# A two-layer cross-attention kernel: the second attention's row maxima two steps earlier, and its tokens turned inside the first MLP

## The reference, cut to what matters

```
x = layer0(x, ctx)                 # 512 queries, 64 keys, 16 heads of 32; then LN, MLP 512->2048->512
# layer 1: queries are the 512 tokens of x ("latents"); keys and values are ctx (64 rows) and x (512 rows)
h = concatenate([ctx, x])
q = latents @ q_w + q_b ; k, v = h @ kv_w + kv_b
p = softmax(where(mask, q k^T / 32, -inf))          # 16 heads, 512 x 576 scores each
y = (p v) @ out_w + out_b + latents
out = gelu(rmsnorm(y) @ mlp_w1 + mlp_b1) @ mlp_w2 + mlp_b2 + latents
```

## Time and profile before

| | us |
|---|---|
| median of 3 runs | 1754.24 (1750.44 to 1754.75) |
| profiled execution, its own time | 1764.97 |
| its span, first to last instruction | 1763.2 |
| attention1 in it | 699 to 1382 |
| mean granted TensorE clock | 0.951 |

### The profile page before, as it was taken

The page is one execution under the profiler, slowest core; times in us unless marked ns, Lnnn a source line. Parts: engine busy times, 40 slices in busy tenths (PEclk is TensorE's granted clock), DMA queues, the critical chain, the costliest instruction groups (busy, mean ns, idle before and its releaser), DMA issues.

```text
span 1763.2 us, 23342 instructions
## 1 busy us (share of the span) xinstructions
PE 1611.1 (91%) x7033; PEld 1212.9 (69%) x7033; DVE 972.0 (55%) x1657; ACT 689.6 (39%) x1243; POOL 556.5 (32%) x543
## 2 busy tenths in 40 slices
PE   5778787989999999899999999999988899999998
PEld 4667675667787777666666666666643677887886
DVE  4665656564333333377757675776787574333333
ACT  3443333342111111178647755883766342111110
POOL 3231236501213140444514433451466401313000
PEclk9788988999999999899999899999986999999999
DMA  5001104500001032723322323322221510001011
GB/s 186 1 30 43 59 24 143 209 13 22 27 18 30 18 115 81 212 66 109 104 76 77 117 64 105 97 86 91 86 74 54 198 36 21 27 16 32 0 48 48
DMA packets 60410, 126.18 MB, mean 72 GB/s; under 512 B 9989, under 2 KB 10378, under 8 KB 60322
## 3 DMA queue, kind: packets, MB, share of 16 engines
q1 hardware_dynamic: 53282, 102.13, 17.5%
q0 software_dynamic: 7040, 23.07, 4.2%
HBM read 90.25 MB, written 34.60 MB: 71 GB/s over the span
## 4 chain that ended last, share of the span: by engine, by line
PE 74%; DVE 12%; issue 6%; ACT 5%; DMA 2%; POOL 0%; SPq 0%; DVEq 0%; ACTq 0%; POOLq 0%
PE bank L2221 19%; PE bank L2233 19%; PE bank L2068 6%; PE bank L2104 4%; DVE RA L1365 4%; PE bank L2119 3%; PE bank L2120 3%; PE bank L2081 3%; PE bank L2128 3%; PE bank L2064 2%; PE bank L1866 2%; PE bank L1890 2%; PE bank L1941 1%; PE bank L1930 1%; DMA RA<-rows_ 1%
## 5 line engine op out<-in xcount | busy, mean ns | idle before, releaser
L2233 PE MATMUL bank<-W,RA 128*128 128x512 f32 x1536 | 379.7, 399 | 5.9 <-DVE RA L1365 5.6
L2221 PE MATMUL bank<-RA,W 128*128 (+1 forms) x1536 | 374.8, 396 | 2.9 <-issue 2.3
L2233 PEld LDWEIGHTS bank<-W,RA 128*128 128x128 f32 x1536 | 287.3, 189 | 78.2 <-DVE RA L1365 10.5
L928 POOL TENSOR_TENSOR RA<-FA,RA 128x512 fp32r<-128x512 f32 (+1 forms) x160 | 233.7, 1463 | 339.7 <-ACT FA L1191 338.7
L2221 PEld LDWEIGHTS bank<-RA,W 128*128 128x128 f32 x1536 | 286.9, 188 | 75.1 <-issue 6.1
L1257 ACT ACTIVATE FA<-bank,cols 128x512 f32<-128x512 f32 x128 | 88.2, 689 | 542.0 <-PE bank L2221 541.9
L1768 DVE CAST RA<-FA 128x512 fp32r<-128x512 f32 x128 | 63.6, 497 | 354.7 <-ACT FA L1257 354.7
L1190 ACT ACTIVATE RA<-bank 128x512 fp32r<-128x512 f32 (+1 forms) x320 | 192.7, 602 | 148.7 <-PE bank L2104 136.3
L1604 DVE TENSOR_REDUCE FA<-bank 128x1 f32<-128x512 f32 x256 | 174.0, 685 | 102.6 <-PE bank L2081 97.1
L1365 DVE TENSOR_TENSOR RA<-FA,RA 128x512 fp32r<-128x512 f32 (+1 forms) x292 | 223.0, 764 | 9.0 <-ACT FA L1191 2.4
L1191 ACT ACTIVATE FA<-bank 128x512 f32<-128x512 f32 (+1 forms) x320 | 191.5, 599 | 0.0
(11 more groups left out here) (154 smaller groups left out, 1829.7 us busy)
## 6 DMA issues: line engine op xcount, KB each, us to landing
RA<-k_parts SPq DMA_DIRECT2D x96, 144.0 KB
FA<-after_layer SPq DMA_DIRECT2D x12, 1024.0 KB, 6.0
RA<-q_parts SPq DMA_DIRECT2D x96, 128.0 KB
k_parts<-FA SPq DMA_DIRECT2D x16, 576.0 KB, 2.8
after_att<-FA SPq DMA_DIRECT2D x32, 256.0 KB, 2.1
q_parts<-FA SPq DMA_DIRECT2D x16, 512.0 KB, 2.6
raw<-in_L_xattn_mlp_w_dram POOLq DMA_DIRECT2D x32, 256.0 KB, 3.4
RA<-after_att SPq DMA_DIRECT2D x10, 512.0 KB, 7.0
```

Of the source, the lines that this page charges most:

```text
L928: pool.tensor_tensor(pl[0:m, r, :], pf[0:m, r, :], ph[0:m, r, :].bitcast(F32), ALU.subtract).then_inc(p_lo_pool, 1)
L2221: op = pe.matmul(bank[FC1_BANK[i]][:, :], W[:, slot, a, k, i * P:(i + 1) * P], yT_[:, ds(b * (2 * KT * S) + (d * KT + k) * S, S)], start=( ...
L2233: op = pe.matmul(bank[4 + t][:, :], gs[:, a, i, t * P:(t + 1) * P], W[:, slot + 1, d, i, :], start=(i == 0 and a == 0 and d == 0), stop=(i ...
```

## The change

Four things are done at once.

1. `SHIFT`, `TURN` = 5, 15 in place of 7, 17: every `max_step` stands two steps earlier, and both rows of maxima are turned two steps earlier. The fillers are laid anew: Q in steps 0 to 3, K in 6 to 11, KC in 12 and 13; in group c = 1 Q in 0 to 3, K in 6 to 8, KC in 9, nC in 17. The opening has 15 max_steps in place of 13.
2. The copy of the turned maxima (`max_turned`) goes from VectorE to ScalarE, ahead of the exponentials of the step after the turn. It waits also for the bank use before it to be freed.
3. TensorE's turning of the tokens leaves attention1. Group 3 of the first MLP is written out in place of a loop, and while batch b (1 to 3) is at work in it, TensorE turns batch b-1 out of `acc_` (`x_turn`, four transposes after each of fc1(1), fc2(0), fc1(2), fc2(1); bank 3), ScalarE moves it out (`x_out`), and SP stores it to the new DRAM tensor `x_turned` (`x_store`); batch 0 goes straight into `xT`, with VectorE writing its lo part (`x_lo`). Batch 3 is turned in the opening, in front of nKC0 and nK1 (banks 2 and 3), stored from there.
4. In group c = 1 the turned tokens of the next batch are loaded into `tokT`; ScalarE writes the hi part (steps 11, 13, 15, 17) and GpSimd the lo part (`x_split`, in its order behind steps 12, 14, 16 and 18) from SBUF. No PSUM bank is used. TensorE waits for the four of them before nQ0, the filler of step 0 of group c = 2.

```diff
-TURN = 17
-SHIFT = 7
+TURN = 15
+SHIFT = 5
...
-    spans = ((0, 3), (3, 3), (8, 1)) if turns else ((0, 6), (8, 6), (14, 2))
+    spans = ((0, 4), (6, 3), (9, 1)) if turns else ((0, 4), (6, 6), (12, 2))
...
-        plan += [(s0, 1, f"nT{k}") for k, s0 in enumerate((9, 11, 13, 15))] + [(18, 1, "nC")]
+        plan += [(s0, 1, f"nT{k}") for k, s0 in enumerate((10, 12, 14, 16))] + [(17, 1, "nC")]
...
-FIRST = ([f"nT{k}" for k in range(KT)] + ["nC", "nQ0", "nK0", "nKC0", "nQ1", "nK1", "nKC1"]
+FIRST = (["nC", "nQ0", "nK0", "nKC0", "nQ1", "nK1", "nKC1"]
...
+FIRST_X = {"nKC0": (0, 1), "nK1": (2, 3)}
...
+            def x_store(nb, k):
+                sp.wait_ge(x_moved, KT * nb + k + 1 + ONE)
+                sp.dma_start(x_turned[nb, :, k, :], x_stage[nb][k]).then_inc(x_stored[k % 2], 16)
...
+                        if not last and n // NSTEP == 1:
+                            for s0, _, u in fillers(1, last):
+                                if u[:2] == "nT" and n % NSTEP == s0 + 2:
+
+                                    k = int(u[2:])
+                                    wait_apart(pool, (act_out, at(0, b, SPLITS, split1(u, last) + 1)))
+                                    pool.tensor_tensor(xT[:, 1, k, :], tokT[:, k, :], xT[:, 0, k, :].bitcast(F32),
+                                                       ALU.subtract).then_inc(x_split, 1)
...
+                def max_turned(b, u, nb, c, pair, last=False, first=False):
+                    n = use1(u, last, first)
+                    wait_apart(act, (pb_full, at(0, b, USES, n + 1)), (pb_free, at(0, b, USES, n)),
+                               (maxed[c % 2][pair], at(0, nb, 32, 16 * (c // 2))))
+                    act.activation(nT[:, c % 2, pair, :], bank[n % 2][0:H // 2, 0:P], ACT.Copy).then_inc(pb_free, 1)
...
+            def x_turn(nb, k):
+
+                if k == 0:
+                    pe.wait_ge(acc_added, (NGRP - 1) * B * TT + (nb + 1) * TT + ONE)
+                pe.wait_ge(x_moved, KT * nb + k - (nb == B - 1 and k > 0) + ONE)
+                for t in range(TT):
+                    at_t = nb * TT * D + t * D + k * P
+                    op = pe.transpose(bank[3 if nb < B - 1 else 2 + k % 2][:, t * P:(t + 1) * P],
+                                      acc_[:, at_t:at_t + P], ident[:, :])
+                op.then_inc(x_full, 1)
...
-                            wait_apart(pe, (pb_free, at(0, b, USES, use1("nC", last) + 1)))
+                            wait_apart(pe, (pb_free, at(0, b, USES, use1("nC", last) + 1)), (x_split, at(0, b, KT, KT)))
```

More of the change, by code:

```diff
@@ L1242, in attention1 @@
                 act.activation(cols[:, NPAR + 3:NPAR + 4], cols[:, NPAR:NPAR + 1], ACT.Exp)
-                for u in split_by_act(FIRST):
-                    hi(0, u, first=True)
+                for u in FIRST:
+                    for k in FIRST_X.get(u, ()):
+                        x_out(B - 1, k)
+                    if u == "nR00":
+                        max_turned(0, u, 0, 0, 0, first=True)
+                    else:
+                        hi(0, u, first=True)
+                for i in range(2):
+                    act.wait_ge(x_stored[i], 16 * (B - 1) * KT // 2 + ONE)
                 with act.Fori(0, B - 1) as b:
@@ L1274, in mlp @@
                 for g in range(1, NGRP):
-                    with act.Fori(0, B) as b:
-                        batch(b, g, False)
+                    if L.index == 0 and g == NGRP - 1:
+                        for b in range(B):
+                            batch(b, g, False)
+                    else:
+                        with act.Fori(0, B) as b:
+                            batch(b, g, False)
             act.wait_ge(consts, 2 + ONE)
@@ L1807, in mlp @@
                 for g in range(1, NGRP):
-                    with dve.Fori(0, B) as b:
-                        batch(b, g, False)
+                    if L.index == 0 and g == NGRP - 1:
+                        for b in range(B):
+                            batch(b, g, False)
+                    else:
+                        with dve.Fori(0, B) as b:
+                            batch(b, g, False)
             attention0()
@@ L2146, in batch @@
                     for c in range(G):
-                        at_step = {s0 + part: (u, part, n) for s0, n, u in fillers(c, last) for part in range(n)}
+                        at_step = {s0 + part: (u, part, n) for s0, n, u in fillers(c, last) for part in range(n)
+                                   if u[:2] != "nT"}
                         turns = max_turns(c, last)
@@ L2268, in mlp @@
                     pe.wait_ge(w_lo, L.before + L.units + (g + 1) * 2 * KT + ONE)
-                    with pe.Fori(0, B) as b:
-                        batch(b, g, False)
+                    if L.index == 0 and g == NGRP - 1:
+                        for b in range(B):
+                            batch(b, g, False)
+                    else:
+                        with pe.Fori(0, B) as b:
+                            batch(b, g, False)
             attention0()
@@ L2309 @@
     parts = [nc.dram_tensor(n, (2, P, 2, m), F32, kind="Internal").ap() for n, m in (("q_parts", S), ("k_parts", NK))]
-    program(nc, *main, weights, *between, *parts, out)
+    x_turned = nc.dram_tensor("x_turned", (B, P, KT, S), F32, kind="Internal").ap()
+    program(nc, *main, weights, *between, *parts, x_turned, out)
     r = run_bass_kernel_spmd(nc, [arrays], core_ids=[0])
```

114 lines of the change are left out of this document (82 added, 32 removed).

## The result

The changed kernel took 1742.15 us (median of 7 runs, 1737.32 to 1745.57) beside 1754.75 us (7 runs, 1750.44 to 1765.5) for the kernel before: ratio 0.9909, interval 0.9886 to 0.9932. It is faster by 0.9%. The forecast was 1729 us, with 1710 to 1744 as its range and faster as the likeliest sign; sign and range held, but the gain was 13 us by the medians (16 by the ratio) and not 25. The profiled executions stand further apart: 1764.97 and 1743.69 us, spans 1763.2 and 1741.8.

The account below looks back on a forecast made before the run. TensorE, busy 91% of the span, was taken to bound the kernel, with waits and lower clock in attention1. Terms -16.6 - 14 - 4.0 + 4.3 - 6 + 11 = -25.3 us, scaled to the median: 1729 us, range 1710 to 1744.

Parts of the forecast that it names:

- My own case: Whole kernel: the six terms together give 1729 us, between 1721 and 1740; chance 0.61.
- rival (b): Attention1: the row waits go but the clock behind them stays low; -11 us, 1743; chance 0.12.
- term 1: Attention1, first score of a group: the eight waits for the row of maxima nearly vanish; -16.6 us.
- term 2: Attention1, behind the eight row waits: TensorE no longer falls to the lower clock; -14 us.
- term 3: Opening: without nT0 to nT3 on the path, nQ0 and what follows start earlier; -4.0 us.
- term 4: First MLP, group 3: the token transposes put in there are paid in full; +4.3 us.
- term 5: Group c = 1, steps 10 to 19: ScalarE alone sets the pace, each of three batches shorter; -6 us.
- term 6: Start of c = 2: nQ0 waits for GpSimd's lo parts in three batches, lower clock behind; +11 us.
- (a): Attention1 group starts: the row stays half on the path, with the lower clock; 1750 us; chance 0.10.
- (c): Start of c = 2: GpSimd keeps up and nQ0 does not wait; -39 us, 1715; chance 0.12.
- (d): Row turns: ScalarE's copy waits for its bank and holds up exponentials; slower, +11 us, 1765; chance 0.05.

Follow-up runs that it names:

- the rows' half alone: Kernel before with points 1 and 2 of the change only, tokens still turned by TensorE in attention1: 1740.36 us, ratio 0.9904.
- the tokens alone: Changed kernel with the old steps and fillers and the row of maxima copied by VectorE: 1764.7 us, ratio 1.0046 to the kernel before.
- second kernel with K in two steps: The rows' half alone, with K's projection in two steps for three and step 5's row issued ahead of the residual's load: 1734.6 us, ratio 0.9868.

## Why the prediction was right, and where its size was off

The direction was right for the reason given: the rows' half alone gives the whole gain. That the range held owes something to luck. My own case was 1721 to 1740, and 1742.15 lies above it; the range reached to 1744 for rival (b), whose mechanism did not come, and the second set of runs of the same kernel had 1744.13.

Measured terms, from the two profiled executions (lengths of groups and gaps in the trace of TensorE):

| | forecast | measured |
|---|---|---|
| term 1, waits for the row | -16.6 | -17.1 + 3.8 = -13.3 |
| term 2, clock behind them | -14 | -16.4 |
| term 3, opening | -4.0 | -2.5 |
| term 4, turning in the MLP | +4.3 | +4.9 |
| term 5, c = 1, steps 10 to 19 | -6 | +0.8 |
| term 6, nQ0 behind GpSimd | +11 | +5.3 |
| layout of c = 2; MLP groups 0 to 2; last part | 0 | +1.4 + 2.0 - 3.2 |
| sum | -25.3 | -21.0 (spans: -21.4) |

**Term 1** was right where it looked: four steps cover the row's way at all eight places, with nothing left of the wait. What it did not see is the row of step 5. It is issued 0.60 us behind the 1 MB load of the residual and the score goes on only 5.6 us after its issue (825.13 to 830.70), where the row at the boundary took 2.35; before, 3.4 us lay between the two issues, and nothing waited. The prediction looked at what SP issues in front of the row for K's store and not for this load. That the load is the reason is shown by the kernels with the row ahead: the waits are gone in all of them.

**Term 2** is the term that decides. In the profiled execution it came as forecast: group c = 1 is 6.6 us shorter in its steps 0 to 9 over three batches, c = 3 with the output 5.5, the last batch 4.3, and the windows show 1.00. (About 1 us of the 6.6 is nT0, three times 0.35, which stood in step 9 before.) The step that was mis-sized is the last one of the sum, "25.3/1764.97 = 1.43% of 1754.24 is 25". It took a share of a long execution off a typical one. The 44 runs of the kernel before in the three groups have a mean clock of 0.957 and a median of 1756.9 us, the profiled one 0.951 and 1764.97; over these the time falls by 1.3 us for each 0.001 of clock (correlation -0.87), and only 2 of 44 were as long as the profiled one. The straight line through them gives 1764.8 us at 0.951, where the profiled one took 1764.97. So most of the 10.7 us between profile and median goes with the lower clock, and a change that removes the lower clock can't give back what a typical run does not lose. The changed kernel's two sets of runs have 0.965 and 0.963. From clock and span, the time lost to the clock is (1 - 0.957) x 1755 = 75 us in a typical run before, 86 in the profiled one, and 61 to 64 after: 11 to 14 us less for a typical run, 25 between the two profiled ones. (This overstates the loss, as it counts the lower clock in idle stretches too; the comparison holds, the sizes do not add up with the table.) This account rests on the timed runs' clocks and is argued; no run tests it by itself. The sum on the profiled execution, 1739.7 against 1743.69, was off by 4. At which of the eight places a typical run keeps its clock can't be told, as only one execution has a trace.

**Term 3**: nQ0 came 4.0 us earlier against the end of the MLP, and so did the first max_step, though the idle stretch before it grew from 7.01 to 7.37 us where the prediction had it 1.5 shorter. But 1.5 us went again in front of the body: with 15 max_steps three of them stand in a row behind nV2's splitting, and two banks don't take three (the wait of 1.44 us at 745.94). The prediction had named GpSimd's loads as the next thing late; it was VectorE.

**Term 4** held: group 3 took 4.9 us longer. The MLP's groups 0 to 2, which the change leaves alone, took 287.3 us before and 288.6 to 291.2 in the others, also in those with the old MLP, so 2 us of the difference are not the change's; what they are is open.

**Term 5** is the step that was wrong in kind. "ScalarE alone sets the pace" left out VectorE. The three stretches took 14.0, 15.5 and 14.0 us against 14.2, where 12.2 was forecast. Two waits of TensorE make the difference: without them batch 0 would have needed 11.9 us. The first is 0.74 us for a bank (800.51): the reduction that frees it stands behind the lo part of K and a finished head in VectorE's order, and none of these was slow. The second is 1.32 us for the join of the maxima (805.44). In front of it stand a subtraction of two SBUF tiles that took 1.63 us and the join itself with 0.78, where 0.68 and 0.17 are usual: 1.56 us later, more than the wait. In batch 1 the clock fell behind that wait (0.74 in the 6.4 us from 960.56), which makes the 15.5.

The Trainium skill (SBUF — State Buffer, "Who interferes with whom") says that a VectorE instruction with two SBUF inputs and a GpSimd instruction that reads SBUF exclude each other. The trace agrees: 0.694 at most with one input in PSUM, 1.833 with both in SBUF. I had weighed that rule for GpSimd's side alone, as a longer wait of nQ0; in these steps the price was paid on VectorE's. The moved work is a part of the cause here: in steps 10 to 19 the timelines show no subtraction over 0.7 us in the kernel before and with the rows alone, but two, one and two over 1.5 us in the changed kernel, and three a batch with the tokens alone, where the join takes 1.30 us. But the kernel with VectorE writing the tokens' lo parts has them as well, so what decides is how the two orders meet, and that was not varied by itself.

**Term 6** was right in kind and too high: 1.96, 1.09 and 1.95 us of waiting, 5.0 in place of 7.5, and the clock behind cost about what it had cost there before (3.4 against 3.1, by the groups' lengths), in place of 3.5 more. GpSimd took 13.0 us for its nine operations, where I had 13.5; but TensorE reached nQ0 1.74 us behind the exponentials of step 18 (811.42 against 809.68) and not 1.0: it had worked without a gap since 805.44, so it and not ScalarE set the pace here. That the wait is loss is likely and not shown: with nQ0 one step later the group is shorter in the trace, but the time is not clear of the changed kernel's.

**The rivals.** (a) did not come in the place it named. (b), the clock staying low, is nearest to the time that was measured (1743), but not by its mechanism. (c) fell with the waits of nQ0. (d) fell twice: ScalarE's copy takes 0.25 us and nothing stood behind it, and on VectorE it costs no more or less.

So the rows' half did what was claimed. The tokens' half paid in two places (4.9 us in an MLP where TensorE had no slack, and the GpSimd wait with VectorE's slow subtractions); beside the rows that is about what it saved, and alone it cost half a per cent.

## What to carry to other kernels

Before a forecast is scaled from a profile to a median, compare the clock of the profiled execution with that of the timed runs: lost clock in a long execution is not there to be won in a typical one. Moving elementwise work from VectorE to GpSimd frees less than it seems where both then read SBUF; ask what the moved work does to the engine it leaves, and look at both engines again after any shift of their orders against each other. And when a small transfer is issued earlier, look at every large one that it now stands behind.

## What the runs showed of the hardware

- A subtraction of two SBUF tiles on VectorE took 0.67 us while GpSimd stood still, and 1.6 to 1.7 us beside it (802.52, 809.29, 812.05); with an input in PSUM 0.694 us was the longest of 112. It can fall the other way: at 808.32 in the kernel before it took 0.67, and GpSimd's instruction beside it 2.00.
- The score waited for a row issued 0.60 us behind a 1 MB load until 5.6 us after the issue; issued ahead, the row held nothing up.
- TensorE fell to the lower clock (matmuls 0.43 us apart) behind gaps of 1.4 us in two of three batches (800.27 in the second kernel with K in two steps) and behind the two of 1.95 and 1.96 us in front of nQ0 (813.38), though it was busy before and after; behind the one of 1.09 us in that place it did not, and behind the 1.3 us in front of the turn of step 15 (805.44) in one batch of three. In the kernel with nQ0 later and the row ahead it fell behind a gap of only 0.74 us (799.53) in two batches of three (0.50 from 802 to 808 us).
- The same kernel's executions differ by up to 1% (1749 to 1769 us in 44), and the time goes with the clock (correlation -0.87).
